# Graph attention and mixture of experts on one core: register loads and first steps of the expert stage in another order

## The chip, the core and the metric

The kernel runs on one core of one Trainium2 chip. The metric is the device time of one execution in microseconds (us). A core has a matrix engine (TensorE, "PE" in the profile, with its weight loads as "PEld"), a vector engine (VectorE, "DVE"), a scalar engine (ScalarE, "ACT"), a general engine (GpSimd, "POOL") and a queue engine that here only issues transfers (SyncE, "SP"). Each has its own instruction stream; they meet through semaphores. A name with a "q" behind it ("PEldq", "ACTq", "DVEq", "POOLq") is the sequencer of that engine, which handles waits, register work and the issue of DMAs.

## What is computed

A graph attention layer over 2048 nodes with 128 features and a dense 0/1 adjacency, and behind it a mixture of 64 experts in which each node goes to its two best experts:

```python
h = ln(x) @ W.T + b_W
e = (h @ a1)[:, None] + (h @ a2)[None, :] + b_a[0]
e = where(e > 0, e, 0.2 * e)
attention = softmax(where(adj > 0, e, -9e15), axis=1)
x = x + attention @ h

logits = ln(x) @ Wr + br                    # (2048, 64)
topk_logits, topk_idx = top_k(logits, 2)
gates = softmax(topk_logits, axis=1)
for e in range(64):
    hid = relu(ln(x) @ W1[e] + b1[e])       # 128 -> 256
    y = hid @ W2[e] + b2[e]                 # 256 -> 128
    out = out + combine[:, e:e + 1] * y     # combine: the gate, or 0
x = x + out
```

## The kernel before

**Attention stage** (about the first 140 us). Sixteen tiles of 128 nodes. DVE forms the scores (L712 to L727), PE turns them (L999), ACT takes the exponential (L569) and PE multiplies with h (L1015). Beside it the routing of finished tiles runs: logits, the two best experts, and each row's place in a table in DRAM, written by POOL with indirect DMAs (L425).

**Between the stages** (about 142 to 167 us). The 4096 rows (two for each node), sorted by expert, are cut into 33 blocks of 128 rows (NB). A pair is a block with an expert that has rows in it: 96 pairs (PAIRS = NB + 63). Small matmuls on PE (L1073 to L1097) work out tables from the counts: where each expert begins, which row of the table each partition gathers (`gidx`), the two sides of each pair's rows within its block (`sides`), the first-layer bias for each pair (`b1_at`, L1097), and for each pair the block's number and the weight slot's number. The last two are packed four to a 32-bit word: 24 words of blocks and 24 of slots (WORDS = 24), which DVE copies into `words` (L872, semaphore `s_tab`). The engines then load them into registers with `load_words` (L306 to L309): `engine.load` is one instruction (L308, TENSOR_LOAD in the profile), `snap` (L309) leaves a few register operations (FUSED_REGOPS, or ISA in a listing of instructions).

POOL gathers a pair of blocks (g = 0 to 16) with each indirect DMA of L475, semaphore `e_g`; from g = 3 on it first waits for `e_xt`, the transposes of an earlier pair of blocks.

**Expert stage** (about 167 to 260 us). Each engine's steps are written out by hand in the order in which they run:

- `take(g)` on PE transposes two gathered blocks (L1106) into a bank, and ACT's `x_evac(g)` copies it to `xT_all` (L623).
- `fetch(p)` on ACT copies the first-layer weights of pair p out of their slot, whose number is in a register, into one of four places (L636).
- `up(p)` on PE is the first layer (L1117: two matmuls of 32-bit floats, shown in the trace as four passes). It waits for `fetch(p)` (`e_w`) and `x_evac` (`e_xts`), and for p of 2 or more for both relus of pair p - 2.
- `relu(p)` runs in halves, on ACT (L628) and on DVE (L884), and adds the bias from `b1p`, which ACT copied from its bank (L619, semaphore `s_b1`).
- `down(p)` on PE is the second layer (L1129, four passes). It reads the slot's number from the registers `slots`, waits for both relus of pair p, and for `e_acc` from pair 4 on.
- `gather(p, b)` on DVE adds the product, masked to the expert's rows, into block b (L891). POOL scales finished blocks (L487, behind a load of one register, L484) and scatters them (L489).

The order on PE before the loop is: wait for the second-layer weights (`d_w2`) and for `s_tab`, load both halves of the words, `take(0)`, `take(1)`, `up(0)`, `up(1)`; then wait for `s_mask` and `s_b1`; then for each p `take` (every second p), `up(p + 2)`, `down(p)`. ACT copies the bias table, waits for the first-layer weights (`d_w1`) and `s_tab`, loads its words, fetches pairs 0 to 2, and evacuates blocks 0 and 1. DVE computes `above` and `mask` (L876, L878) and loads its words behind them. A sequencer runs ahead of its engine's data path until a wait holds it.

**Behind it**: PE transposes the gates and multiplies them with b2, SP loads the scattered result back, DVE adds and SP stores.

Of the kernel before, what the change touches and what calls it, by code (L numbers as in the profile page):

```python
# [6 lines left out]
def build(nc, x, adj, weights, biases, w1, b1, w2, b2, out):  # L7
    F32, BF16, I32, U32 = mybir.dt.float32, mybir.dt.bfloat16, mybir.dt.int32, mybir.dt.uint32
    ALU, ACT = mybir.AluOpType, mybir.ActivationFunctionType
# [7 lines left out]
    HB = HID // P  # L17
# [19 lines left out]
    UW, RING, LATE = 4, 48, 4  # L37
    PACK = 4
    WORDS = -(-PAIRS // PACK)
    TAB = PACK * WORDS  # L40
    assert TOPK * E == P and TAB <= P and NB <= 64 and E <= 64
    EPS = 1e-5
    SLOPE = 0.2
# [7 lines left out]
    with ctx:  # L51
        def sb(name, shape, dt=F32):
            return ctx.enter_context(nc.sbuf_tensor(name, shape, dt))
# [36 lines left out]
        hT = carve(UH * HB * P).rearrange("p (u b i) -> p u b i", u=UH, b=HB)  # L90
        b1p = carve(HB * TAB).rearrange("p (b i) -> p b i", b=HB)
        words = carve(2 * WORDS).bitcast(I32).rearrange("p (k i) -> p k i", k=2)[0:1, :, :]
        above, mask = (carve(TAB) for _ in range(2))
        w_later, w_here = (carve(NG2)[0:E, :] for _ in range(2))
# [26 lines left out]
        before_f, upto_f, upto_h = (sb(f"{k}_f", [E + 1, E]) for k in ("before", "upto", "upto_half"))  # L121
        steps_i = sb("steps_i", [P, TAB + NB + NG2], I32)
        steps = sb("steps", [P, TAB + NB + NG2])
        pair_of, block_at, slot_at = steps[0:E, 0:TAB], steps[0:E, TAB:TAB + NB], steps[:, TAB + NB:TAB + NB + NG2]
        part = sb("part", [E, P])
# [56 lines left out]
        ends, coded, sides, b1_at = bank[0][0:E, 0:3], bank[4][0:1, 0:2 * WORDS], bank[5], bank[3][:, 0:HB * TAB]  # L182
# [9 lines left out]
        d_w2 = sem("d_w2")  # L192
# [62 lines left out]
        s_tp = sem("s_tp")  # L255
        s_tab = sem("s_tab")
# [6 lines left out]
        s_b1 = sem("s_b1")  # L263
# [42 lines left out]
        def load_words(engine, name, k, i0, i1):  # L306
            regs = [engine.alloc_register(f"{name}{i}") for i in range(i0, i1)]
            engine.load(regs, words[0:1, k, i0:i1])  # L308
            return [engine.snap(r, min_val=0, max_val=64 ** PACK - 1) for r in regs]  # L309
# [184 lines left out]
        def _(act):  # L494
# [120 lines left out]
                act.activation(y_all[:, b0:b1_, :],  # L615
                               ident[:, :].rearrange("p (b d) -> p b d", b=1).to_broadcast([P, b1_ - b0, D]), ACT.Copy, scale=0.0).then_inc(s_zero, 1)

            act.wait_ge(s_tp, 6)
            act.activation(b1p[:, :, :], b1_at.rearrange("p (b i) -> p b i", b=HB), ACT.Copy).then_inc(s_b1, 1)  # L619

            def x_evac(g):
                act.wait_ge(e_xt, g + 1)
                act.activation(xT_all[:, 2 * P * g:2 * P * g + 2 * P].rearrange("p (h j i) -> p h j i", h=2, j=2),  # L623
                               xp(g).rearrange("p (j h i) -> p h j i", h=2, j=2), ACT.Copy).then_inc(e_xts, 1)
# [13 lines left out]
            act.wait_ge(d_w1, 16 * (RING // HEAD))  # L638
            act.wait_ge(s_tab, 1)
            slots = load_words(act, "act_u", 1, 0, WORDS)  # L640
            for p in range(UW - 1):
                fetch(p)
            act.wait_ge(s_b1, 1)
            x_evac(0)
            x_evac(1)
            for p in range(PAIRS):
                relu(p)
                if p % 2 == 1 and p // 2 + 2 < NG2:
# [11 lines left out]
        def _(dve):  # L660
# [210 lines left out]
            dve.wait_ge(s_tp, 4)  # L871
            dve.tensor_copy(words, coded.rearrange("p (k i) -> p k i", k=2)).then_inc(s_tab, 1)  # L872

            dve.wait_ge(s_tp, 5)
            lo, hi = (sides[:, k * P:k * P + TAB] for k in range(2))
            dve.tensor_scalar(above, lo, sidx[:, :], None, ALU.is_le).then_inc(s_above, 1)  # L876
# [14 lines left out]
                dve.scalar_tensor_tensor(y, yp(p), mask[:, p:p + 1], y, ALU.mult, ALU.add).then_inc(e_acc, 1)  # L891

            dve.wait_ge(s_zero, 2)
            dve.wait_ge(s_tab, 1)
            blocks = load_words(dve, "dve_b", 0, 0, WORDS)
            dve.wait_ge(s_b1, 1)
            relu(0)
            relu(1)
# [40 lines left out]
        def _(pe):  # L939
# [161 lines left out]
            def take(g):  # L1101
                pe.wait_ge(e_g[g % UG], 16 * (g // UG + 1))
                if g >= 2:
                    pe.wait_ge(e_xts, g - 1)
                for j in range(2):
                    ins = pe.transpose(xp(g)[:, j * P:(j + 1) * P], rows_in[:, g, j, 0:D], ident[:, :])  # L1106
                ins.then_inc(e_xt, 1)

            def up(p):
                pe.wait_ge(e_w, p + 1)  # L1110
                pe.wait_ge(e_xts, min(p, NB - 1) // 2 + 1)
                if p >= 2:
                    pe.wait_ge(e_ha, p - 1)
                    pe.wait_ge(e_hb, p - 1)
                column = block_of(blocks, p) * P
                for b in range(HB):
                    ins = pe.matmul(hp(p, b), w1u[:, p % UW, P * b:P * b + P], xT_all[:, bass.ds(column, P)], start=True, stop=True)  # L1117
                ins.then_inc(e_h, 1)
# [11 lines left out]
                                    start=(b == 0), stop=(b == HB - 1))  # L1130
                ins.then_inc(e_y, 1)

            pe.wait_ge(d_w2, 16 * 8)
            pe.wait_ge(s_tab, 1)
            blocks = load_words(pe, "pe_b", 0, 0, WORDS)
            slots = load_words(pe, "pe_u", 1, 0, WORDS)
            take(0)
            take(1)
            up(0)
            up(1)  # L1140
            pe.wait_ge(s_mask, 1)
            pe.wait_ge(s_b1, 1)
            for p in range(PAIRS):
                if p % 2 == 0 and p // 2 + 2 < NG2:
                    take(p // 2 + 2)
                if p + 2 < PAIRS:
                    up(p + 2)
                down(p)
# [44 lines left out]
```

## Time and profile before

| | us |
|---|---|
| Median of 3 runs | 273.82 |
| Lowest and highest | 273.25, 275.77 |
| Span of the profiled execution | 278.2 |
| PE busy in it | 221.1 |
| DVE busy | 219.3 |
| ACT busy | 173.6 |
| POOL busy | 167.4 |

The profile is one execution, 4.4 us longer than the median of the timed runs. Its times are counted from the first instruction, and durations are taken from it. "Granted clock" is the share of TensorE's full rate that the chip granted: 1.00 is its level of 2.4 GHz and 0.50 its level of 1.2 GHz; the mean over this span is 0.920. Register, branch and semaphore instructions are not counted as busy, but the trace shows them with the sequencers.

### The profile page before, as it was taken

The page shows a single profiled execution, that of the slowest core. Times are in us where ns is not written, and L with a number is a line of the kernel's source. Part 1 is how long each engine was busy: PE and PEld are TensorE (multiplying, and loading weights), DVE is VectorE, ACT ScalarE, POOL GpSimd, SP SyncE. Part 2 cuts the span into 40 slices and gives each one's busy share as a digit, 9 for nine tenths or more (in the row PEclk, how much of TensorE's full clock was granted, in tenths as well). Part 3 has the DMA queues.
Part 4 walks back from the last instruction along what each step waited for, and adds up shares of the span by engine and source line. Part 5 has one row for each costly group of instructions (what it writes and reads, how often), then busy time and mean ns, then how long its engine had stood idle before and what let it go on. Part 6 is the DMA issues. An engine that isn't in the chain of part 4 may idle for free.

```text
span 278.2 us, 6188 instructions
## 1 busy us (share of the span) xinstructions
PE 221.1 (79%) x1849; PEld 211.8 (76%) x1849; DVE 219.3 (79%) x628; ACT 173.6 (62%) x393; POOL 167.4 (60%) x194
## 2 busy tenths in 40 slices
PE   1493998989677878869933369999999999999840
PEld 1263998989677877869933249999999999999740
DVE  6899999999999999998866413889887666666464
ACT  2758777978665868658415025878876777777400
POOL 5770007163788588888667344445888888866600
PEclk9998699999999999979995556999999999999995
DMA  6989744876649607019911122222149710100067
GB/s 157 202 164 171 139 76 75 194 194 184 164 85 252 224 26 294 31 26 375 416 45 48 36 57 57 61 66 72 51 133 319 252 40 31 40 28 24 31 199 262
DMA packets 11119, 36.88 MB, mean 133 GB/s; under 512 B 2256, under 2 KB 2832, under 8 KB 10320
## 3 DMA queue, kind: packets, MB, share of 16 engines
q0 software_dynamic: 5232, 14.98, 24.6%
q1 hardware_dynamic: 5424, 21.11, 21.7%
q10 hardware_dynamic: 432, 0.40, 0.6%
q8 instruction: 17, 0.28, 0.4%
q14 instruction: 14, 0.11, 0.1%
HBM read 39.36 MB, written 5.51 MB: 161 GB/s over the span
## 4 chain that ended last, share of the span: by engine, by line
PE 45%; DVE 33%; issue 9%; DMA 5%; another core or an unknown queue 2%; ACT 1%; POOL 1%; SPq 1%; ACTq 1%; POOLq 0%; DVEq 0%
PE bank L1117 17%; PE bank L1129 15%; DVE arena L721 8%; DVE arena L727 7%; PE bank L1015 4%; PE bank L999 3%; DVE arena L712 3%; DMA arena<-result 2%; DMA xs<-in_x 2%; DVE xs L735 2%; DVE st L738 2%; PE bank L1106 1%; DVE xs L808 1%; DVE idx L758 1%
## 5 line engine op out<-in xcount | busy, mean ns | idle before, releaser
L1015 PE MATMUL bank<-arena 128*128 128x130 f32 x512 | 62.7, 279 | 1.9 <-ACT arena L569 1.9
L1015 PEld LDWEIGHTS bank<-arena 128*128 128x128 f32 x512 | 60.4, 194 | 2.6 <-DVE xs L735 1.5
L1117 PE MATMUL bank<-arena 128*128 x384 | 61.3, 284 | 0.6 <-ACT arena L623 0.5
L1129 PE MATMUL bank<-w2s,arena 128*128 x384 | 59.2, 277 | 0.2 <-issue 0.2
L425 POOL DMA_INDIRECT table<-rows_in,pos x32 | 48.0, 1501 | 11.4 <-issue 8.1
L1117 PEld LDWEIGHTS bank<-arena 128*128 128x128 f32 x384 | 52.0, 197 | 1.4 <-issue 1.3
L1129 PEld LDWEIGHTS bank<-w2s,arena 128*128 128x128 f32 x384 | 51.2, 194 | 0.6 <-issue 0.6
L891 DVE SCALAR_TENSOR_TENSOR arena<-bank,arena 128x128 f32 x96 | 33.6, 350 | 22.2 <-PE bank L1129 15.2
L628 ACT ACTIVATE arena<-bank,arena 128x128 f32<-128x128 f32 x96 | 35.2, 367 | 19.8 <-PE bank L1117 15.4
L999 PE MATMUL bank<-ident,arena 128*128 128x128 f32 x256 | 33.8, 290 | 13.9 <-DVE arena L727 13.9
L999 PEld LDWEIGHTS bank<-ident,arena 128*128 128x128 f32 x256 | 30.5, 149 | 15.1 <-DVE arena L727 15.1
L569 ACT ACTIVATE arena<-bank 128x512 f32<-128x512 f32 x64 | 33.7, 596 | 12.1 <-PE bank L999 12.1
L636 ACT ACTIVATE arena<-arena 128x256 f32 x96 | 39.0, 408 | 2.3 <-issue 2.2
L489 POOL DMA_INDIRECT result<-arena x33 | 33.7, 1021 | 9.2 <-POOL arena L487 8.9
L884 DVE TENSOR_SCALAR arena<-bank,arena 128x128 f32<-128x128 f32 x96 | 33.2, 346 | 7.4 <-PE bank L1117 7.0
L727 DVE SCALAR_TENSOR_TENSOR arena<-arena,tneg 128x2048 f32<-128x2048 f32 x16 | 37.3, 2334 | 0.0
L721 DVE CUSTOM_DVE_ANT_0 arena<-arena 128x2048 f32<-128x2048 bf16 x16 | 36.5, 2284 | 0.0
L559 ACT ACTIVATE arena<-arena,c_lo 128x2048 f32<-128x2048 f32 x16 | 32.1, 2004 | 0.5
L475 POOL DMA_INDIRECT rows_in<-table,arena x17 | 16.2, 953 | 22.4 <-PE bank L1106 15.5
L374 POOL DMA_DIRECT2D arena<-in_adj x16 | 9.3, 583 | 28.2 <-DVE arena L712 27.8
L487 POOL TENSOR_SCALAR arena<-arena 128x128 f32<-128x128 f32 x32 | 19.7, 616 | 6.7 <-DVE arena L891 5.5
L575 ACT ACTIVATE rows_in<-xs,nm,rstd 128x256 f32<-128x256 f32 x16 | 8.8, 595 | 17.8 <-POOL nm L410 17.7
(193 smaller groups left out, 273.9 us busy)
## 6 DMA issues: line engine op xcount, KB each, us to landing
arena<-in_adj POOLq DMA_DIRECT2D x16, 512.0 KB, 5.4
w2s<-in_w SPq DMA_DIRECT2D x8, 768.0 KB, 4.9
arena<-in_w SPq DMA_DIRECT2D x6, 1024.0 KB
arena<-in_w SPq DMA_DIRECT2D x4, 512.0 KB
w2s<-in_w SPq DMA_DIRECT2D x4, 512.0 KB
xs<-in_x SPq DMA_DIRECT2D x4, 256.0 KB, 6.5
arena<-result SPq DMA_DIRECT2D x2, 512.0 KB, 4.3
arena<-result SPq DMA_DIRECT2D x4, 256.0 KB, 6.1
```

The costliest lines, as they stand in the source:

```text
L425: pool.indirect_dma_start(table[:, :], bass.IndirectOffsetOnAxis(pos[:, t, k:k + 1], 0), rows_out[:, t, k, :].bitcast(I32), None).then_inc ...
L489: pool.indirect_dma_start(result[:, :], bass.IndirectOffsetOnAxis(slot_id[:, b:b + 1], 0), y_all[:, b, :], None).then_inc(e_put, 16)
L569: act.activation(pt_r[:, t % 2, CB * b:CB * b + CB, :].rearrange("p c i -> p (c i)"), bank[b][:, :], ACT.Exp, scale=-1.0).then_inc(s_ea, 1)
L628: act.activation(hT[:, p % UH, 0, :], hp(p, 0), ACT.Relu, bias=b1p[:, 0, p:p + 1]).then_inc(e_ha, 1)
L636: act.activation(w1u[:, p % UW, :], w1s[:, bass.ds(u, 1), :].rearrange("p e h -> p (e h)"), ACT.Copy).then_inc(e_w, 1)
L721: dve.tensor_tensor_reduce(out=z_r[:, t % 3, :], in0=pen[:, t % 2, :], in1=trow[:, :], scale=1.0, scalar=HIGHEST, op0=ALU.add, op1=ALU.min ...
L727: dve.scalar_tensor_tensor(z, z, tneg[:, t:t + 1], low(t), ALU.subtract, ALU.min).then_inc(s_lk, 1)
L891: dve.scalar_tensor_tensor(y, yp(p), mask[:, p:p + 1], y, ALU.mult, ALU.add).then_inc(e_acc, 1)
L999: ins = pe.transpose(bank[b][:, P * c:P * c + P], z_r[:, t % 3, P * j:P * j + P], ident[:, :])
L1015: ins = pe.matmul(OB[t % 2][:, 0:D + 2], pt_r[:, t % 2, j, :], h[:, j, :], start=(j == 0), stop=(j == T - 1))
L1117: ins = pe.matmul(hp(p, b), w1u[:, p % UW, P * b:P * b + P], xT_all[:, bass.ds(column, P)], start=True, stop=True)
L1129: ins = pe.matmul(yp(p), hT[:, p % UH, b, :], w2s[:, bass.ds(u, 1), b, :].rearrange("p e d -> p (e d)"), start=(b == 0), stop=(b == HB - 1))
```

## The change

Five steps are put in another order, and one is split in two. No arithmetic is changed, and every wait for data is kept, some of them later in their queue.

- PE loads the block words first, then does `take(0)` and `take(1)`, then loads only the first 4 slot words (those of pairs 0 to 15), then `up(0)` and `up(1)`. The wait for `d_w2` stands behind `up(1)`.
- PE loads the other 20 slot words at the top of the loop's second pass (p = 1), ahead of `up(3)` and `down(1)`.
- ACT loads its words and fetches pairs 0 and 1 before it waits for the bias table and copies it; then it evacuates block pairs 0 and 1, and then fetches pair 2.
- DVE loads its block words right behind the copy that makes them, ahead of `above` and `mask`.

```diff
--- before.py
+++ after.py
@@ -38,6 +38,7 @@
     PACK = 4
     WORDS = -(-PAIRS // PACK)
     TAB = PACK * WORDS
+    FIRST = 4
     assert TOPK * E == P and TAB <= P and NB <= 64 and E <= 64
     EPS = 1e-5
     SLOPE = 0.2
@@ -615,9 +616,6 @@
                 act.activation(y_all[:, b0:b1_, :],
                                ident[:, :].rearrange("p (b d) -> p b d", b=1).to_broadcast([P, b1_ - b0, D]), ACT.Copy, scale=0.0).then_inc(s_zero, 1)
 
-            act.wait_ge(s_tp, 6)
-            act.activation(b1p[:, :, :], b1_at.rearrange("p (b i) -> p b i", b=HB), ACT.Copy).then_inc(s_b1, 1)
-
             def x_evac(g):
                 act.wait_ge(e_xt, g + 1)
                 act.activation(xT_all[:, 2 * P * g:2 * P * g + 2 * P].rearrange("p (h j i) -> p h j i", h=2, j=2),
@@ -638,11 +636,15 @@
             act.wait_ge(d_w1, 16 * (RING // HEAD))
             act.wait_ge(s_tab, 1)
             slots = load_words(act, "act_u", 1, 0, WORDS)
-            for p in range(UW - 1):
+            fetch(0)
+            fetch(1)
+            act.wait_ge(s_tp, 6)
+            act.activation(b1p[:, :, :], b1_at.rearrange("p (b i) -> p b i", b=HB), ACT.Copy).then_inc(s_b1, 1)
+            x_evac(0)
+            act.wait_ge(s_b1, 1)
+            x_evac(1)
+            for p in range(2, UW - 1):
                 fetch(p)
-            act.wait_ge(s_b1, 1)
-            x_evac(0)
-            x_evac(1)
             for p in range(PAIRS):
                 relu(p)
                 if p % 2 == 1 and p // 2 + 2 < NG2:
@@ -871,6 +873,9 @@
             dve.wait_ge(s_tp, 4)
             dve.tensor_copy(words, coded.rearrange("p (k i) -> p k i", k=2)).then_inc(s_tab, 1)
 
+            dve.wait_ge(s_tab, 1)
+            blocks = load_words(dve, "dve_b", 0, 0, WORDS)
+
             dve.wait_ge(s_tp, 5)
             lo, hi = (sides[:, k * P:k * P + TAB] for k in range(2))
             dve.tensor_scalar(above, lo, sidx[:, :], None, ALU.is_le).then_inc(s_above, 1)
@@ -891,8 +896,6 @@
                 dve.scalar_tensor_tensor(y, yp(p), mask[:, p:p + 1], y, ALU.mult, ALU.add).then_inc(e_acc, 1)
 
             dve.wait_ge(s_zero, 2)
-            dve.wait_ge(s_tab, 1)
-            blocks = load_words(dve, "dve_b", 0, 0, WORDS)
             dve.wait_ge(s_b1, 1)
             relu(0)
             relu(1)
@@ -1130,17 +1133,19 @@
                                     start=(b == 0), stop=(b == HB - 1))
                 ins.then_inc(e_y, 1)
 
-            pe.wait_ge(d_w2, 16 * 8)
             pe.wait_ge(s_tab, 1)
             blocks = load_words(pe, "pe_b", 0, 0, WORDS)
-            slots = load_words(pe, "pe_u", 1, 0, WORDS)
             take(0)
             take(1)
+            slots = load_words(pe, "pe_u", 1, 0, FIRST)
             up(0)
             up(1)
+            pe.wait_ge(d_w2, 16 * 8)
             pe.wait_ge(s_mask, 1)
             pe.wait_ge(s_b1, 1)
             for p in range(PAIRS):
+                if p == 1:
+                    slots += load_words(pe, "pe_u", 1, FIRST, WORDS)
                 if p % 2 == 0 and p // 2 + 2 < NG2:
                     take(p // 2 + 2)
                 if p + 2 < PAIRS:
```

PE, from the last matmuls of the tables to `up(1)`; `b_s` is the bias, `w2s` the second-layer weights, `rows_in` the gathered rows. Before:

```order
L1097 MATMUL bank<-r_hot,b_s 128x96 x2
L308 TENSOR_LOAD arena [waits s_tab,d_w2]
L309 ISA x3
L308 TENSOR_LOAD arena
L309 ISA x3
L1106 MATMUL bank<-ident,rows_in 128x128 [waits e_g0]
L1106 MATMUL bank<-ident,rows_in 128x128
L1106 MATMUL bank<-ident,rows_in 128x128 [waits e_g1]
L1106 MATMUL bank<-ident,rows_in 128x128
L1117 ISA [waits e_xts,e_w]
L1117 MATMUL bank<-arena 128x128 x2
```

The same place now (all lines of the changed kernel are shifted by 1 to 5):

```order
L1100 MATMUL bank<-r_hot,b_s 128x96 x2
L309 TENSOR_LOAD arena [waits s_tab]
L310 ISA x3
L1109 MATMUL bank<-ident,rows_in 128x128 [waits e_g0]
L1109 MATMUL bank<-ident,rows_in 128x128
L1109 MATMUL bank<-ident,rows_in 128x128 [waits e_g1]
L1109 MATMUL bank<-ident,rows_in 128x128
L309 TENSOR_LOAD arena
L310 ISA
L1120 ISA [waits e_xts,e_w]
L1120 MATMUL bank<-arena 128x128 x2
```

The second load with its register operations moved behind the four transposes, and one register operation is left of its three. The other two stand a few rows on, in PE's loop, between `down(0)` and `up(3)`:

```order
L1132 MATMUL bank<-w2s,arena 128x128
L309 TENSOR_LOAD arena
L310 ISA x2
L1120 ISA [waits e_ha,e_hb,e_xts,e_w]
L1120 MATMUL bank<-arena 128x128 x2
```

ACT, from the bias table's copy to the first relu, before:

```order
L619 ACTIVATE arena<-bank 128x192 [waits s_tp]
L308 TENSOR_LOAD arena [waits s_tab,d_w1]
L309 ISA x3
L636 REGISTER_ALU
L636 ACTIVATE arena<-arena 128x256
L636 ISA
L636 ACTIVATE arena<-arena 128x256
L636 ISA
L636 ACTIVATE arena<-arena 128x256
L623 ACTIVATE arena<-bank 128x256 [waits e_xt,s_b1]
L623 ACTIVATE arena<-bank 128x256 [waits e_xt]
L628 ACTIVATE arena<-bank,arena 128x128 [waits e_h]
```

And now, where L642 is the bias table's copy, L634 `fetch` and L621 `x_evac`:

```order
L309 TENSOR_LOAD arena [waits s_tab,d_w1]
L310 ISA x3
L634 REGISTER_ALU
L634 ACTIVATE arena<-arena 128x256
L634 ISA
L634 ACTIVATE arena<-arena 128x256
L642 ACTIVATE arena<-bank 128x192 [waits s_tp]
L621 ACTIVATE arena<-bank 128x256 [waits e_xt]
L621 ACTIVATE arena<-bank 128x256 [waits e_xt,s_b1]
L634 ISA
L634 ACTIVATE arena<-arena 128x256
L626 ACTIVATE arena<-bank,arena 128x128 [waits e_h]
```

The load no longer stands behind the wait for `s_tp`, which the bias table's copy took with it; the third fetch went behind both evacuations.

## Rows read from the trace of the kernel before

**Rows 1.** Stretches in us: busy and count by engine, PEclk, DMA share, GB/s.

```profile
core 0: us, PE busy (x) PEld busy (x) DVE busy (x) ACT busy (x) POOL busy (x), PEclk, DMA share, GB/s
165.00:168.00 3.00, 1.69 (x6) 1.30 (x7) 0.00 (x0) 1.57 (x5) 0.95 (x1) 0.50 0.01 3
168.00:172.00 4.00, 4.00 (x20) 4.00 (x20) 1.16 (x4) 2.40 (x7) 1.90 (x2) 0.50 0.30 75
172.00:176.00 4.00, 4.00 (x37) 4.00 (x36) 3.32 (x12) 2.82 (x9) 1.54 (x2) 0.96 0.20 60
250.00:260.00 10.00, 9.98 (x89) 9.80 (x87) 6.95 (x23) 6.48 (x19) 5.66 (x8) 1.00 0.07 23
```

**Rows 2.** The chain that ended last, in order of time: start, length, what.

```profile
162.38 0.88 issue
163.32 1.69 ACTq L308
...
165.80 0.17 ACT arena L636
...
166.74 0.64 ACT arena L623 x2
167.38 0.04 issue
167.42 2.07 PE bank L1117 x8
169.49 0.43 PE bank L1106 x2
...
171.63 0.84 PE bank L1117 x4
...
173.13 0.45 PE bank L1117 x4
```

**Rows 3.** Line L308, the register loads: ns min/median/max, first and last start.

```profile
L308 PEldq TENSOR_LOAD <-arena x2: 1624/1716/1807, 161.0 to 163.5; - x2
L308 DVEq TENSOR_LOAD <-arena x1: 1856/1856/1856, 163.1 to 163.1; - x1
L308 ACTq TENSOR_LOAD <-arena x1: 1689/1689/1689, 163.3 to 163.3; - x1
```

**Rows 4.** Lines L309 and L484, the same columns: register operations, loads of one word.

```profile
L309 PEldq FUSED_REGOPS  x6: 100/175/188, 162.8 to 165.6; - x6
L484 POOLq TENSOR_LOAD <-arena x32: 283/289/514, 193.8 to 259.1; - x32
```

**Rows 5.** Timeline of 160 to 170 us: start, length, instruction, idle before it.

```profile
161.50 0.97 POOL L475 DMA_INDIRECT rows_in<-table,arena  x1 [0.30 <-issue]
162.16 1.06 PE L1097 MATMUL bank<-r_hot,b_s 64*128 64x96 f32 x4
162.41 0.32 DVE L876 TENSOR_SCALAR arena<-bank,sidx 128x96 f32<-128x96 f32 x1 [1.57 <-PE bank L1095]
163.26 0.33 ACT L619 ACTIVATE arena<-bank 128x192 f32<-128x192 f32 x1 [10.61 <-PE bank L1095]
165.79 1.11 PE L1106 MATMUL bank<-ident,rows_in 128*128 128x128 f32 x4 [2.57 <-issue]
165.80 1.03 ACT L636 ACTIVATE arena<-arena 128x256 f32 x3 [2.21 <-issue]
168.68 0.37 ACT L628 ACTIVATE arena<-bank,arena 128x128 f32<-128x128 f32 x1 [1.31 <-PE bank L1117]
169.28 0.64 PE L1106 MATMUL bank<-ident,rows_in 128*128 128x128 f32 x2
```

**Rows 6.** Two stretches with the landings of gathers 0 and 1, columns as above.

```profile
161.80:162.80 1.00, 1.00 (x5) 1.00 (x6) 0.36 (x2) 0.00 (x0) 0.69 (x2) 0.50 0.46 133
163.10:164.10 1.00, 0.12 (x1) 0.00 (x0) 0.00 (x0) 0.33 (x1) 0.63 (x1) 0.50 0.56 133
```

**Rows 7.** PE's sequencer: wait for the words, wait ahead of up(0), down(0), up(3).

```profile
L1134 PEldq EVENT_SEMAPHORE  x1: 51/51/51, 160.9 to 160.9; - x1
L1111 PEldq EVENT_SEMAPHORE  x1: 51/51/51, 167.1 to 167.1; - x1
L1129 PEldq FUSED_REGOPS  x2: 62/78/93, 169.6 to 169.8; - x2
L1113 PEldq EVENT_SEMAPHORE  x1: 51/51/51, 169.9 to 169.9; - x1
```

## The prediction, made before the changed kernel ran

> **What bounds the kernel now.** I read the stretches first, to see where PE is the bound and where it is not. From 168 us on PE is busy 4.00 us in every 4.00, and at the end of the expert stage still 9.98 in 10.00; from 165 to 168 it is busy for only 1.69 of 3.00 [rows 1]. So once the first `up` has started, PE never again waits for anybody until the pairs are done, and all behind it (the last scatter, the load of the result, the store) hangs on its last pair. Whatever brings the first `up` forward brings the end forward by the same amount, unless PE gets a new hole.
>
> Then the chain in order of time, to see what the first `up` waits for [rows 2]. It starts at 167.42. Ahead of it stand an evacuation by ACT, ACT's first fetch at 165.80, ACT's register load of 1.69 us at 163.32, and ahead of that the wait for the bias table's matmuls. PE is no better off: its own two register loads begin at 161.0 and 163.5 [rows 3], its register operations end just ahead of the first transpose, at 165.79, and before that it sat idle for 2.57 us for "issue", that is for its own sequencer [rows 4, 5]. Two chains of nearly equal length thus end at the first `up`: ACT's (bias copy, load, three fetches, evacuations) and PE's (load, load, transposes, evacuation). The change shortens both, and DVE's mask lies beside them.
>
> The last fact is the clock. The granted clock is 0.50 (the 1.2 GHz level) from 165 to 172 us and 0.96 in the next 4 us [rows 1]; four passes of an `up` cost 0.84 us at the low level and 0.45 at the high one (2.4 GHz) [rows 2]. By the mean of 0.96 the rise falls at 172.3, 4.9 us after the first `up`. Each us of PE work at the low level therefore costs about 0.47 us.
>
> **What a register load costs.** The trace has loads of 24 words, 1.62 to 1.86 us [rows 3], and of one word on POOL, 0.29 us [rows 4]. It has none of 4 or 20. A straight line between them gives (1.62 - 0.29) / 23 = 0.058 to (1.86 - 0.29) / 23 = 0.068 us for each further word: 0.48 us for 4 words, and 1.4 to 1.6 us, taken as 1.5, for 20. The bounds are the neighbours: 4 words between 0.29 and 1.62, 20 words between 0.29 and 1.86. I take the line, because both ends of it are on the same chip in the same kernel, though on different engines.
>
> A rule speaks against the change here. By the Trainium skill (Runtime: NRT & Kernel Launch, Instruction fetch mechanics) a register load takes about 200 ns for each register even in bulk. By that page 24 words would take 4.8 us, where the rows have 1.62 to 1.86, or 68 to 77 ns a word. By the page the 4 words would cost 0.8 and the 20 words 4.0 us, and the sum below would turn from a gain into a loss of some 1 us. The measurement decides; what is left of the doubt is rival 5.
>
> **PE's side of the first up.** The wait for `s_tab` passes at 160.9 [rows 7] and the first load starts at 161.0, while the data path is still busy with the tables until 162.16 + 1.06 = 163.22 [rows 5]; so a load does run under matmuls that are already queued. The second load started at 163.5. In its place `take(0)` now goes: 163.5 instead of 165.79. Gather 0 has landed by 162.8 [rows 6]. `take(1)` needs gather 1, issued at 161.50 [rows 5], whose packets lie between 163.1 and 164.1 [rows 6]; so its transposes go at about 164.1 and are dispatched by 164.2. Then the load of 4 words, 0.48, and one register operation, 0.18 [rows 4]: 164.9. From the semaphore wait of `up(0)` to its first matmul it took 167.42 - 167.1 = 0.3 [rows 2, 7]: **165.2**.
>
> **ACT's side.** The load can start when PE's does, at 160.9. From load to first fetch the old order took 165.80 - 163.32 = 2.48 [rows 2]: first fetch at 163.4. Three fetches took 1.03 [rows 5], so two are issued in 0.7: 164.1. The bias table is ready at 163.26 and is copied in 0.33 [rows 5]: 164.4. `x_evac(0)` needs the transposes of 163.5, which take 0.64 for one pair of blocks [rows 5], 164.1, so it is ready; 0.37 more (two took 0.64 together) [rows 2]: 164.8, and with the 0.3 of the wake **165.1**. PE's own load is later by a hair, so `up(0)` goes at 165.2, **2.2 us earlier** than 167.42.
>
> **What I cost at nothing, and its cover.** The third fetch moves behind `x_evac(1)`: that waits for `take(1)`, 164.2 + 0.64 = 164.8, ends at about 165.2, and the fetch at 165.6. `up(2)` wants it when relu(0) is done, 169.05 - 2.2 = 166.9 by 168.68 + 0.37 [rows 5]; 1.3 us of cover. DVE's load at 160.9 pushes the mask from 162.41 [rows 5] to 160.9 + 1.86 + 0.6 = 163.4, done by 164.1; behind it on DVE nobody waits before relu(0), and PE asks for it at about 165.6; cover 1.5 us, and without it PE would lose what is missing. The wait for `d_w2` costs nothing where it was, nor where it is. POOL's gather 3 is released by the first transposes, so it goes earlier too, and its queue of gathers and scatters shifts with PE.
>
> **The second part of the slot words.** Between `down(0)` and `up(3)` PE's sequencer now has 1.5 us of load and two register operations of 0.2. In the old time scale it finished `down(0)` at about 169.9, when it came to the wait of `up(3)` [rows 7], while the data path reached `up(3)` only at 171.63 [rows 2]: 1.7 us of lead. Now the wait comes at 169.9 + 1.5 + 0.4 = 171.8 and the matmuls 0.3 later, 172.1. The data path runs dry for **0.5 us**, and PE has no slack to win that back. Bounds: no hole if the load takes under 1.0, 0.9 us if it takes 1.86.
>
> **Sum.** 2.2 - 0.5 = 1.7 us gained. The profiled execution of 278.2 would be 276.5; the median of the timed runs, 4.4 us below it, goes from 273.82 to **272.1**, as I take the gain to be the same in us. That is 0.6%, less than the 1% or so that a measurement of this kernel can tell from no change.
>
> **Rivals.**
> 1. *A load has a fixed cost, not one by the word.* For it: 24 words differ by 0.24 us between engines with no cause in the count [rows 3]. Against it: one word takes 0.29 on POOL. If 4 words cost 1.62, `up(0)` goes at 166.3 (gain 1.1), and 20 words at 1.86 make the hole 0.9: gain 0.2, time 273.6. Chance 0.15.
> 2. *The hole keeps the clock low (the one on the other side).* Place: PE's data path, ahead of `up(3)`. In the old order PE ran without a gap from 167.42, and the clock rose 4.9 us later. If a gap makes that count start again, it rises 4.9 us after the hole's end: the low stretch is then 4.2 us of work before the hole plus 4.9, 9.1 instead of 4.9. 4.2 x 0.47 = 2.0 us, more than the whole gain: 274.1. It decides as soon as the low stretch grows by over 1.7 / 0.47 = 3.6 us. Against it: the hole is short, and the stretch of 165 to 168 had a gap as well. Chance 0.13. Only with the dearer loads of rival 1 and a rise later still would it pass 276.5; of the 0.13 that has 0.02.
> 3. *The clock comes back sooner.* PE's work begins at 163.5 with the transposes and goes on from 165.2, so the rise may come 2 us or more earlier relative to the first `up` than now. 1 to 2 us less at the low level give 0.5 to 0.9: 271.2 to 271.6, and with no hole 270.7. Chance 0.17.
> 4. *The change doesn't do what it says*, because another wait holds the first `up`, say gather 1 under other traffic or the copy of `b1p`. The gathers' rows speak against it. Time 273.5 to 273.8. Chance 0.05.
> 5. *A long load inside the loop is far dearer than a line through the rows*, for instance because PE's sequencer loads while the other engines work. A 20-word load of 4 us makes a hole of 0.5 + 2.5 = 3.0 us, and the time is 273.82 - 2.2 + 3.0 = 274.6. Against it: PE's load at 161.0 ran beside its own matmuls and took 1.8 at most [rows 3]. Chance 0.02. This is where the Trainium skill's price (Runtime: NRT & Kernel Launch) would lead.
>
> The forecast has the remaining 0.48, with 271.4 to 272.8 as its own range.
>
> **How the numbers follow.** The range leaves out 1 in 10 at each side. Down to 270.6: ACT's 165.1 as the start (gain 2.3), no hole, and an earlier clock (0.9, rival 3). Up to 274.4: rivals 1, 2 and 4 are all below that, as is the spread of the timed runs of before except their highest. Faster by over 1% means below 271.08: most of it the better half of rival 3 with a small hole, and the luck of the measurement, 0.13. Slower by over 1% means above 276.56: 0.03. The rest, 0.84, is within 1%.
>
> **What would show each step.** In the profile of the changed kernel, against the same time of `s_tab`: PE's first transposes some 2.3 us earlier; the first `up` 4.3 us after PE's wait for `s_tab`, where it was 6.5; a load of 4 words near 0.5 us and one of 20 near 1.5; a gap of 0.5 us on PE ahead of `up(3)`; the granted clock back at 1.00 some 5 us after the first `up`. A first `up` that comes 2 us earlier with an end that does not would mean that the hole or the clock took the gain. What would make it wrong: a 4-word load over 1 us, a mask or a third fetch that PE waits for, or waits ahead of the expert stage, untouched by the change, that come out otherwise in the timed runs.

## The result: 0.5% slower, and a usual execution has another bound

| | kernel before | changed kernel |
|---|---|---|
| Median of 16 runs, us | 273.75 | 275.24 |
| Lowest and highest | 272.79, 275.77 | 273.94, 276.85 |
| Span of the profiled execution | 278.2 | 272.5 |

The ratio is 1.0049, with a 95% interval of 1.0025 to 1.0073: slower by 1.3 us by the ratio (1.5 between the medians), where 1.7 us of gain had been forecast, and above the range of 270.6 to 274.4.

The spans of the two profiled executions say the opposite, and that is the first thing to explain. Every run here lists its time and its span, and the time is about 1.85 us longer (274.35 and 272.5 for the profiled run of the changed kernel). By that a span of 278.2 belongs to a time of some 280.0, which none of the 16 timed runs of before came near. The profile on which the prediction was built was of an unusual execution.

The changed kernel's chain, in order of time (start, length, what):

```profile
152.40 0.96 POOL table L426
153.36 0.30 issue
153.66 2.15 DMA table<-padrow,pad_at
...
155.88 0.75 issue
156.63 1.00 POOL rows_in L476
157.64 0.30 issue
157.94 2.82 DMA rows_in<-table,arena
160.76 0.05 issue
160.81 0.69 PE bank L1109 x2
161.50 0.15 issue
161.65 2.07 PE bank L1120 x8
163.72 0.43 PE bank L1109 x2
164.15 0.83 PE bank L1120 x4
```

Up to the first `up` no register load and nothing of ACT is in it. POOL writes the last rows into the table (L426), then the padding row, which has landed 2.15 us after the start of its issue, gathers blocks 0 and 1 (156.63) and then blocks 2 and 3 (157.94), and 2.82 us after that second start `take(1)` can go. The first `up` (L1120) is at 161.65. In [rows 2] the same place was ACT's load, fetches and evacuations.

PE's stretches of the changed kernel (busy and count by engine, PEclk, DMA share, GB/s), which answer to [rows 1]:

```profile
158.00:162.00 4.00, 1.72 (x5) 0.93 (x6) 0.11 (x1) 1.11 (x5) 3.03 (x4) 0.50 0.36 100
162.00:166.00 4.00, 3.41 (x18) 3.22 (x17) 1.38 (x5) 2.68 (x8) 1.66 (x2) 0.65 0.26 67
166.00:170.00 4.00, 3.57 (x32) 3.58 (x33) 2.46 (x10) 2.14 (x7) 0.94 (x1) 1.00 0.19 49
170.00:174.00 4.00, 4.00 (x39) 4.00 (x38) 3.32 (x13) 3.23 (x11) 1.89 (x2) 1.00 0.20 57
```

Two of these stretches in the kernel before, from the second profile of it that is told of below:

```profile
162.00:166.00 4.00, 4.00 (x31) 4.00 (x31) 2.05 (x7) 2.86 (x9) 1.89 (x2) 0.81 0.33 87
166.00:170.00 4.00, 4.00 (x38) 4.00 (x38) 3.34 (x13) 3.23 (x11) 1.89 (x2) 1.00 0.25 69
```

After the first `up` PE now lacks 0.59 us in one stretch and 0.43 in the next. The hole is one piece, in PE's timeline:

```profile
164.79 0.62 PE L1132 MATMUL bank<-w2s,arena 128*128 x4
166.43 0.71 PE L1120 MATMUL bank<-arena 128*128 x4 [1.02 <-ACT arena L634]
```

The row names ACT's fetch (L634 in the changed kernel, L636 before) as the releaser, but that ended at 165.68. What ended last was PE's own sequencer, which these rows of the lines of `load_words` show (ns min/median/max, start). The load of 20 words runs from 164.2 to 165.57, its last register operation ends at 165.98, and PE ran dry at 164.79 + 0.62 = 165.41:

```profile
L309 PEldq TENSOR_LOAD <-arena x1: 346/346/346, 160.8 to 160.8; - x1
L309 PEldq TENSOR_LOAD <-arena x1: 1367/1367/1367, 164.2 to 164.2; - x1
L310 PEldq FUSED_REGOPS  x2: 180/180/180, 165.6 to 165.8; - x2
```

### The profile page after: what moved, and what is told of

Its sections match the earlier page's. It is cut to its first block, busy times and chain, and to the rows that moved or that the text cites. A ratio compares the mean times of both kernels' runs of the same rounds, so it can differ in the third digit from the quotient of the medians.

```text
span 272.5 us, 6188 instructions
## 1 busy us (share of the span) xinstructions
PE 220.2 (81%) x1849; PEld 210.6 (77%) x1849; DVE 219.2 (80%) x628; ACT 173.5 (64%) x393; POOL 166.8 (61%) x194
## 4 chain that ended last, share of the span: by engine, by line
PE 41%; DVE 31%; issue 11%; DMA 7%; POOL 6%; SPq 1%; ACT 1%; POOLq 0%; DVEq 0%
PE bank L1120 17%; PE bank L1132 16%; DVE arena L723 9%; DVE arena L729 7%; POOL table L426 4%; PE bank L1018 3%; DVE arena L714 3%; PE bank L1002 2%; DMA arena<-result 2%; DMA xs<-in_x 2%; DVE xs L737 2%; DVE st L740 2%; PE bank L1109 2%; DMA rows_in<-table,arena 1%; DVE xs L810 1%
## 5 line engine op out<-in xcount | busy, mean ns | idle before, releaser
L1120 PE MATMUL bank<-arena 128*128 x384 | 60.8, 282 | 1.3 <-ACT arena L634 1.0
L426 POOL DMA_INDIRECT table<-rows_in,pos x32 | 48.0, 1499 | 10.3 <-issue 8.3
L1120 PEld LDWEIGHTS bank<-arena 128*128 128x128 f32 x384 | 51.6, 196 | 2.1 <-issue 2.1
L634 ACT ACTIVATE arena<-arena 128x256 f32 x96 | 39.1, 408 | 6.2 <-issue 6.1
```

Source lines behind the costliest of these rows:

```text
L426: pool.indirect_dma_start(table[:, :], bass.IndirectOffsetOnAxis(pos[:, t, k:k + 1], 0), rows_out[:, t, k, :].bitcast(I32), None).then_inc ...
L634: act.activation(w1u[:, p % UW, :], w1s[:, bass.ds(u, 1), :].rearrange("p e h -> p (e h)"), ACT.Copy).then_inc(e_w, 1)
```

## The experiments

Each ratio below is to runs of the kernel before that were taken beside that kernel, with its 95% interval; each profile is of one execution.

### The kernel before, profiled again

> The kernel before, unchanged, profiled once more. Theory G (the gathers set the start of the expert stage): the profiled execution of before was not a usual one, it had two waits of DVE of 2.4 and 2.9 us ahead of the tables that the changed kernel's profile has not. Then this profile has a span near 272, s_tab near 154.8, the first gather at 156.6 behind the landing of the last put, the first transposes near 159.6 to 160.4 and the first up at 161.2 to 161.7, no later after s_tab than in the changed kernel (7.0 us). Theory L (the register loads set it, as forecast): the waits of DVE come again in most executions, the span is near 277, the first up stands 6.5 us behind the wait for s_tab with PE's loads last. Time: ratio 1.00 by both.

Ratio 0.9984 (0.9958 to 1.0011), median 273.13, profiled span 270.5. Its chain:

```profile
153.45 2.15 DMA table<-padrow,pad_at
...
156.42 1.00 POOL rows_in L475
157.43 0.30 issue
157.73 2.80 DMA rows_in<-table,arena
160.54 0.04 issue
160.58 0.69 PE bank L1106 x2
161.27 0.05 issue
161.32 2.07 PE bank L1117 x8
163.39 0.36 PE bank L1106 x2
163.75 0.44 PE bank L1117 x4
```

This is the changed kernel's chain, piece for piece, up to the first `up`. The first `up` is 4.90 us behind the start of the first gather here and 5.02 in the changed kernel: the reordering did not bring it forward. Its register loads are where they were, in relation to the words, but they end before gather 1 lands:

```profile
L308 PEldq TENSOR_LOAD <-arena x2: 1628/1718/1808, 154.9 to 157.5; - x2
```

The second load starts at 157.5, so with their register operations both are over at about 159.7. `take(0)` stood right behind them, at 159.79, which is 3.37 us after the first gather's start, where the changed kernel needed 2.87. But `take(1)` then waited for gather 1 until 160.58, and that wait covered the loads.

The missing piece is on DVE: the copy of the words ran at 154.53, where the first profile had it at 160.64. The chain of the first profile had two waits of DVE there, of 2.4 and 2.9 us:

```profile
151.34 2.42 another core or an unknown queue
154.41 2.91 another core or an unknown queue
```

This one has no idle time at the first place, and 0.77 us at the second:

```profile
151.24 0.15 DVE L850 TENSOR_SCALAR mark<-bank 64x3 f32<-64x3 f32 x1 [0.77 <-PE bank L1079]
```

Together the two waits are 4.6 us longer than here (5.33 less 0.77), of the 6.1 us by which the copy was later. They held the tables and the first gather back, gave the puts time to land, and so let both register loads start late and stand last. Theory G (the gathers) got its numbers here (span 270.5, copy at 154.53, first `up` at 161.32), theory L (the loads) did not. What caused the two waits stays open.

### Delaying the gathers

```diff
+            for _ in range(2):          # 8 in pool_later_before, 20 in gathers_late_*
+                link(pool.memset(iota_i[:, :], 0))
             pool.wait_ge(s_gidx, 1)
```

> The kernel before with two extra memsets of a 128x128 int32 table on POOL, chained, just ahead of the first gather; they compute nothing that is used. Theory G (the gathers set the first up): the whole delay is passed on. The distance from the copy of the words to the first up, 6.8 us in the second profile of before, grows by what the memsets take beyond the landing of the last put, and the time with it. If POOL's wait for that landing (2.15 us) swallows them, nothing moves. Theory L (the register loads set it): the distance stays 6.8 us, since the loads are still there and the gathers have slack.

> The kernel before with eight chained memsets of 0.24 us and their 0 to 0.3 us between them ahead of the first gather, where two had been hidden under the landing of the last put. Theory G: what they take beyond that landing, 2 us or so, is passed on in full: first up 8.5 to 9 us after the copy of the words instead of 6.8, time 275.0 to 276.0. Theory L: 273.5 to 274, since the register loads and not the gathers would be last.

Most of both was covered by the landing of the last put: 2 memsets took 0.48 us, moved nothing and cost nothing (0.9983, 0.9956 to 1.0010); 8 took 2.06 us, moved the first gather by 0.6 us against the padding row, and cost too little to be seen (1.0011, 0.9989 to 1.0034). The first `up` came 7.18 us behind the copy of the words, where theory G had 8.5 to 9, so neither kernel decides. Twenty memsets do:

> The kernel before with 20 chained memsets on POOL ahead of the first gather (0.26 us each, 5.1 us together; eight of them had moved the first gather by only 0.6 us). Theory G: the first gather starts 3.7 us later than in before, and the first up follows it by 4.5 to 4.9 us as ever, so the time is 3.5 us above before, 277.0 to 277.8. Theory L: the register loads would cover the delay at least in part, first up less than 2 us later.

> The changed kernel with the same 20 memsets. Theory G: all of the new order's earlier steps wait for the gathers, its first up follows the first gather by 5.0 us as in the changed kernel, the hole of the in-loop load stays, and it is 1 to 1.8 us slower than gathers_late_before. If the new order were worth anything where gathers are late, it would be no slower.

POOL's timeline of the kernel before with the delay:

```profile
154.53 0.91 POOL L464 DMA_INDIRECT table<-padrow,pad_at  x1 [0.30 <-issue]
155.43 5.20 POOL L467 MEMSET iota_i<- 128x128 int32 x20
161.27 1.00 POOL L477 DMA_INDIRECT rows_in<-table,arena  x1 [0.64 <-POOL iota_i L467]
```

From the padding row to the first gather it is 6.74 us instead of 2.97, 3.8 more, and from the padding row to the first `up` 11.38 instead of 7.87, 3.5 more. So all of the gathers' delay but 0.3 us is passed on to the first `up`. The time agrees, 277.24 instead of 273.78, though four runs leave it wide (ratio 1.0133, 1.0056 to 1.0209, which is 1.5 to 5.7 us). The changed kernel under the same delay takes 279.29 (1.0196, 1.0138 to 1.0255), 2.0 us more than the old order where 1 to 1.8 had been expected: where the gathers are last, the new order is only a cost.

### The forecast's own state, made on purpose

```diff
+            for _ in range(12):
+                link(dve.memset(rk[:, :, :, :], 0.0))
             dve.wait_ge(s_tp, 2)
```

> The kernel before with 12 chained memsets of a dead table on DVE ahead of the copy that starts the tables: the state that the first profile of before had by its two long waits (there about 5 us, here 3 to 4.5). By both theories the tables, the gathers and the words then come late together, the landed puts no longer matter, and the register loads stand on the path as in the forecast: first up 6.5 to 6.8 us after the copy of the words, the gathers' landings ahead of the transposes. Time: before plus what the delay is beyond the puts' landing, 1 to 3 us.

> The changed kernel with the same 12 memsets. If the forecast's chain was right for the state that it was read from, the first up comes 4.5 to 4.8 us after the copy of the words here against 6.5 to 6.8 in the same state of the kernel before, and the hole ahead of up(3) takes back 0.5 to 1.0 of that: this kernel is 0.7 to 1.7 us faster than late_tables_before. If the arithmetic of the chain was wrong too, the first up gains less than 1 us and this kernel is not faster than late_tables_before.

The chain of the kernel before with late tables is that of [rows 2] again:

```profile
164.81 1.68 ACTq L308
...
168.22 0.65 ACT arena L623 x2
168.87 0.04 issue
168.91 2.07 PE bank L1119 x8
```

Its words were copied at 162.12, its first `up` came 6.79 us later. With the new order the words were copied at 161.85 and the first `up` ran at 166.37, 4.52 us later. That is 2.27 us gained; the forecast said 2.2. With the loads out of the way the gathers are last here too: this first `up` is 4.97 us behind the first gather, and every kernel with the load of 4 words has 4.92 to 5.02. Then the hole came, 0.58 us:

```profile
169.72 0.85 PE bank L1134 x4
170.57 0.58 issue
171.15 0.71 PE bank L1122 x4
```

The forecast had 0.5. Medians were 280.82 and 280.09 (ratios to before 1.0245, 1.0193 to 1.0298, and 1.0238, 1.0181 to 1.0295, four runs each), so the new order may be some 0.7 us better in this state; the intervals don't settle it. So two terms of the sum, 2.2 and 0.5, were sound for the execution from which they were read; that they add up to 1.7 us of time is not shown, since the two profiled spans differ by 0.7 (279.1 and 278.4). The clock took a part: the old order's matmuls were at the high level 3.3 us after the first `up` (172.25), the new order's only behind the hole. And this is not the usual execution.

### Which part costs the time

`split_alone` is the kernel before with PE's part of the diff and nothing of ACT's and DVE's. `unsplit` is the changed kernel with PE's loads put back:

```diff
             blocks = load_words(pe, "pe_b", 0, 0, WORDS)
+            slots = load_words(pe, "pe_u", 1, 0, WORDS)
             take(0)
             take(1)
-            slots = load_words(pe, "pe_u", 1, 0, FIRST)
...
-                if p == 1:
-                    slots += load_words(pe, "pe_u", 1, FIRST, WORDS)
```

> The kernel before with PE's new order and its split load alone; ACT and DVE as before. Theory G: the hole and the 4-word load are there in full, 1.0 to 1.5 us slower than before, 274.8 to 275.3. Rival C: about as fast as before, since the cost would lie in ACT's and DVE's order.

> The changed kernel with PE's 24 slot words loaded in one piece right behind the block words, ahead of take(0), as before; ACT's and DVE's new order kept. Theory G: both loads hide under the gathers, the hole of 1.0 us ahead of up(3) is gone and so are the 4-word load and its register operation between take(1) and up(0), so the time falls back to that of before or up to 0.5 us below it: 273.3 to 273.8 against 275.2. Theory L: PE's first up goes later by 1.1 us or more because the loads stand on its path again, the hole's 1.0 us comes back, and the time stays near 275.

`split_alone` has the loss, 1.0038 (1.0010 to 1.0067); `unsplit` does not show it, 1.0015 (0.9990 to 1.0040). The two intervals overlap, but both were measured against the same runs, and their medians are 275.03 and 273.90. PE is busy without a gap again in `unsplit`:

```profile
162.00:166.00 4.00, 4.00 (x26) 4.00 (x26) 1.47 (x5) 3.13 (x10) 2.02 (x3) 0.68 0.25 67
```

So ACT's and DVE's new order is worth nothing that can be measured, and PE's part carries the loss. Within PE's part, the in-loop load was added to the kernel before by itself:

```diff
             for p in range(PAIRS):
+                if p == 1:
+                    slots = slots[:FIRST] + load_words(pe, "pe_v", 1, FIRST, WORDS)
```

> The kernel before with one instruction group added and nothing else: at p = 1 PE loads the last 20 slot words a second time, into other registers, which are used from there on. It measures the in-loop load by itself. Theory H (the hole is the cost of the change): 1.2 to 1.9 us slower than before, 275.0 to 275.6, with a gap of 0.5 to 1.2 us on PE ahead of up(3). Rival (the cost lies elsewhere, in the 4-word load or the other order): within 0.4 us of before.

One added load of 20 words costs 1.0039 (1.0015 to 1.0062), 1.1 us by the ratio where 1.2 to 1.9 had been expected; its gap on PE is 0.90 us:

```profile
165.08 0.73 PE L1130 MATMUL bank<-w2s,arena 128*128 x4
166.72 0.71 PE L1118 MATMUL bank<-arena 128*128 x4 [0.90 <-ACT arena L637]
```

By the two ratios that is most of the change's loss, though their intervals are too wide for a share. The load of 4 words between `take(1)` and `up(0)` adds a little: the six profiles that have it there show the first `up` 4.92 to 5.02 us behind the first gather, the six of the old place (all slot words ahead of `take(0)`, gathers last) 4.64 to 4.90.

### Other places for the load

`rest_after_up1` puts the load of 20 words right behind `up(1)` and takes it out of the loop, `split_at_8` has it at p = 8:

```diff
             up(1)
             pe.wait_ge(d_w2, 16 * 8)
+            slots += load_words(pe, "pe_u", 1, FIRST, WORDS)
```

> The changed kernel with the 20 slot words loaded right behind up(1) instead of in the loop, where PE's sequencer has 1.5 us before relu(0) lets it go on. Theory G: no hole ahead of up(3), the 4-word load stays on the path: 1.0 us better than the changed kernel, 274.2. Rival C (the clock or the new order on ACT costs the time, not the hole): no better than 275.0.

> The changed kernel with the 20-word load at p = 8 instead of p = 1. By then the granted clock is at its high level. If all of the loss is the hole itself, it stays or grows, since PE's queued work at the high level covers only half as long: hole 1.0 to 1.3 us, time 275.0 to 275.5. If the hole at p = 1 also cost time by holding the clock low, that part (0.4 to 1 us) is gone: 274.3 to 274.9.

Neither place is free. `rest_after_up1` was expected 1.0 us better than the changed kernel and is not: 1.0082 (1.0051 to 1.0113). Its gap is smaller, 0.41 us, but stands ahead of `take(2)`:

```profile
164.20 2.07 PE L1120 MATMUL bank<-arena 128*128 x8 [0.25 <-issue]
166.69 0.66 PE L1109 MATMUL bank<-ident,rows_in 128*128 128x128 f32 x2 [0.41 <-issue]
```

Why it is no better than the changed kernel with half its gap I can't show. The intervals of the two overlap, so it isn't shown to be worse either. In its profile the first gather came 2.6 us later than in the changed kernel's, which lies ahead of everything that was moved and came with a lower clock in the attention stage (0.53 from 120 to 125 us and 0.79 from 125 to 130, against 0.66 and 1.00). `split_at_8` is 1.0053 (1.0035 to 1.0071), with a gap of 1.27 us at the high clock:

```profile
173.08 0.61 PE L1132 MATMUL bank<-w2s,arena 128*128 x4
174.96 0.41 PE L1109 MATMUL bank<-ident,rows_in 128*128 128x128 f32 x2 [1.27 <-issue]
```

The load starts at 172.9 and PE runs dry at 173.08 + 0.61 = 173.69, so 0.8 us of it are covered, where the changed kernel had 1.2 (164.2 to 165.41): the queued passes take about half the time at the high level. The part that I thought the clock would give back at p = 8 did not show.

### An earlier first up by other means

If gather 1 is last and `up(0)` reads only blocks 0 and 1, `take(1)` can go behind. Both kernels load all slot words ahead of `take(0)`. On ACT, `x_evac(1)` goes behind the third fetch in `take1_late` and behind `relu(0)` in `take1_mid`:

```diff
             take(0)
             up(0)
+            take(1)        # take1_mid; in take1_late behind up(1)
             up(1)
```

> The changed kernel with all slot words loaded ahead of take(0) as before, and with take(1) moved behind up(1) on PE and x_evac(1) behind the third fetch on ACT: blocks 0 and 1, all that up(0) and up(1) can read, come with gather 0. Theory G: the first up no longer waits for gather 1, whose landing ends 1.3 us after gather 0's; it follows take(0) by about 1.3 us, at 4.2 to 4.5 us after the start of the first gather instead of 4.9, and with no hole in the loop the kernel is 0.3 to 0.8 us faster than before, 273.0 to 273.5. Theory L: no gain, 273.8 or more.

> take1_late mended: take(1) stands between up(0) and up(1) on PE, and ACT evacuates it behind relu(0), so that relu(0) no longer queues behind a wait for take(1). All slot words are loaded ahead of take(0). If the gathers set the first up and nothing else is in the way: first up 4.6 us after the start of the first gather instead of 4.9 to 5.0, no gap ahead of up(2), time 273.0 to 273.5, 0.2 to 0.7 below before, at the edge of what can be measured. If take1_late lost by something other than ACT's queue (a gap of 0.7 us ahead of up(2) and 7 us more at the low clock), this one is at 275 or more as well.

`take1_late` lost, 1.0072 (1.0037 to 1.0107). ACT's `x_evac(1)` stood ahead of `relu(0)` and now waited for a transpose behind both ups, so that ACT's half of `relu(0)` ran at 164.34 and DVE's at 162.88. `up(2)` waited for it:

```profile
165.14 1.22 PE L1120 MATMUL bank<-arena 128*128 x4 [0.69 <-ACT arena L634]
```

The clock then stayed at 0.50 from 166 to 170 us, and PE got 21 passes done there, against 38 in the same stretch of the kernel before. `take1_mid` has no such queue. Its PE has no gap, and it is 1.0012 (0.9987 to 1.0037), not to be told from before. Its profile had a granted clock of 0.50 from 162 to 166 and 0.83 from 166 to 170, where before had 0.81 and 1.00.

Nor did either bring the first `up` forward as expected. It came 4.70 and 4.69 us behind the first gather, where 4.2 to 4.5 and 4.6 had been forecast and `unsplit`, with `take(1)` in its old place, has 4.70. With gather 1 out of the way PE's two loads of 24 words are last: `take(0)` starts 3.27 and 3.26 us after the first gather, against 2.87 in the changed kernel, which has one load there. No version here beats the kernel before.

Three distances in each profile, in us: from the start of the first gather to the first `up`, from there to the end of the last `down`, and PE's gap within the second:

| kernel | to first `up` | to last `down` | gap | ratio of times |
|---|---|---|---|---|
| before, second profile | 4.90 | 92.4 | none | 0.9984 |
| pool_late_before | 4.78 | 93.0 | none | 0.9983 |
| pool_later_before | 4.66 | 93.9 | none | 1.0011 |
| take1_mid | 4.69 | 94.3 | none | 1.0012 |
| unsplit | 4.70 | 92.7 | none | 1.0015 |
| gathers_late_before | 4.64 | 93.0 | none | 1.0133 |
| split_alone | 4.92 | 94.2 | 0.84 | 1.0038 |
| load_added | 4.77 | 94.1 | 0.90 | 1.0039 |
| changed kernel | 5.02 | 94.0 | 1.02 | 1.0049 |
| split_at_8 | 4.97 | 94.7 | 1.27 | 1.0053 |
| rest_after_up1 | 5.00 | 93.5 | 0.41 | 1.0082 |
| take1_late | 4.70 | 96.5 | 0.69 | 1.0072 |
| gathers_late_after | 4.97 | 96.3 | 0.58 | 1.0196 |
| before, first profile | 7.23 | 93.8 | none | |
| late_tables_before | 7.24 | 93.4 | none | 1.0245 |
| late_tables_after | 4.97 | 94.7 | 0.58 | 1.0238 |

One profile does not order kernels this close: without any gap the second distance is anything from 92.4 to 94.3, as the clock comes back earlier or later. Less its gap, each kernel with one lies in that same range, but for `take1_late` and `gathers_late_after` (95.8 and 95.7), whose clocks came back latest.

## Why the prediction was wrong, by its own steps

- **What bounds the kernel.** This is the step that failed. "Two chains of nearly equal length thus end at the first `up`", ACT's and PE's, was true of the profiled execution alone. In a usual one a third chain, puts, their landing, gather 0, gather 1, is last, and both of the others end under it: the first `up` stands 4.90 us behind the first gather in the old order and 5.02 in the new. It was to be seen: the profiled span exceeded even the highest timed run, and that with a time still longer than the span. I took 4.4 us off as a constant ("as I take the gain to be the same in us") where the two waits of DVE just ahead of the change were most of the difference (a span of 278.2 belongs to a time 6.2 us above the median, not 4.4). The last paragraph named "waits ahead of the expert stage" as what could make it wrong, and gave them no chance.
- **PE's and ACT's side, 2.2 us.** Right for late tables, 2.27 measured. In a usual execution there is no gain; the load of 4 words even makes it a little later.
- **Price of a register load.** 4 words 0.35 us (forecast 0.48), 20 words 1.37 (1.5), 24 words 1.62 to 1.91 over all engines and profiles. The line through the neighbours was a little dear. Rival 1 (fixed cost) and rival 5 (far dearer in the loop) are out: 68 ns a word at 20 words. The Trainium skill (Runtime: NRT & Kernel Launch, Instruction fetch mechanics) has about 200 ns for each register even in bulk; this case's trace does not agree.
- **The hole, 0.5 us.** 1.02 in the changed kernel, 0.90 in `load_added`, 0.58 with late tables. The mechanism was right, but this term was mis-sized where the clock had come back before the hole. The matmuls of `up(3)` came 4.78 us after the first `up` (forecast 4.7), but PE ran dry after 3.76 instead of 4.2, since the four passes of `down(0)` took 0.43 us instead of 0.85. I had priced the cover at the low clock only.
- **What I cost at nothing** held: the third fetch, the mask, `d_w2` and the bias copy are in no chain of the changed kernel up to its first `up`.
- **Rival 2, the hole and the clock.** A late return behind a hole does occur, though that the hole caused it is not shown: with the gathers late, the changed kernel's clock was still at 0.50 from 170 to 174 us, where the old order had 1.00:

```profile
170.00:174.00 4.00, 3.48 (x16) 3.48 (x17) 1.59 (x6) 1.14 (x4) 0.70 (x1) 0.50 0.12 33
```

  In the changed kernel's own profile the clock averaged 0.65 from 162 to 166, against 0.81 before, and 0.68 in `unsplit`, which has no hole. How much of the 1.3 us is the clock's is not separated: `split_at_8` was to do it and had a longer hole. The mean clocks of whole runs speak against a clock that is lost more often: they fall into two groups, and 9 of the changed kernel's 16 runs are in the lower (0.928 to 0.929, median 275.79) and 6 in the upper (0.944 to 0.946, 274.62), against 27 (0.929 to 0.932, 274.01) and 16 (0.938 to 0.942, 272.74) of the 44 runs of the kernel before that go with its second profile. (One run of each lies between.) It is slower in both, and has no larger share in the lower.
- **Rival 3, the clock comes back sooner.** It came back 3.3 us after the first `up` in the changed kernel (`up(2)` at 164.15 took 0.83 us, `down(0)` from 164.98 took 0.43), where the forecast had 4.9 from the first profile. But in the second profile of before `up(2)` ran at the high level already 2.4 us after it, so this is no gain of the new order.
- **Rival 4**, "another wait holds the first `up`, say gather 1", is what happened, at a chance of 0.05 and priced at no loss. I looked for it in the rows of the one execution in which the gathers were early, and I did not join it with the hole, which stays when the gain goes: 273.82 + 0.5 = 274.3 would have been its price.

## What to carry to other kernels

Hold the profiled execution's time against the timed runs before reading its chain; if it lies outside them, the waits that make it longer may have moved the bound, and the chain is that of another program. An edit that shortens one of several chains meeting at a point, and pays with a hole where the bounding engine has no slack, is a bet whose cost is surer than its gain. Work of a sequencer is free only where its engine waits for data: here ahead of the first transposes, and at none of the three places behind the first `up` that were tried.

## What the runs showed that I had not expected

- A register load costs nearly by the word: 0.29 us for one on POOL, 0.35 for 4, 1.37 for 20 and 1.62 to 1.90 for 24 on PE, so some 0.064 us for each word more between 4 and 20. In the changed kernel the 24-word loads of PE, DVE and ACT all start at 154.9 and take 1.84, 1.85 and 1.68 us; in the second profile of before PE's first one ran by itself and took 1.81.
- The last put had landed 2.15 us after the start of its issue, and 0.75 us more passed before the gather behind it started. Of 2.1 us of other work that POOL was given there, all but 0.6 us vanished in this.
- At the same place of the program the granted clock returned to 1.00 after very different amounts of work, with and without a gap: PE's passes from 166 to 170 us were 38 in the kernel before and 32 in `take1_mid`.
- The granted clock also fell in some executions at 120 us, in the attention stage: its mean from 120 to 125 us was 0.66 in the changed kernel's profile and 1.00 in the second profile of before. That is ahead of everything that was moved. In the six profiles with this fall and no long delay added (the changed kernel, `load_added`, `split_alone`, `split_at_8`, `rest_after_up1`, `pool_late_before`) the first gather starts at 156.6 to 159.2, in four without it (the second of before, `unsplit`, `take1_mid`, `take1_late`) at 156.4 to 157.0.
